# Two edits in a four-pass feed-forward kernel: the transposed loads of the next pass are issued after the gate stage, and the weight casts come in batches of 20 instead of 16

## The reference

```
x = layernorm(x + conv(x, filt))          # a 2048-tap filter along the sequence, D = 1024
g = silu((x @ w1.T) * s1) * ((x @ w2.T) * s2)      # 1024 -> 4096
u = gelu((g @ h1.T) * sh1)                         # 4096 -> 4096
v = gelu((u @ h2.T) * sh2)                         # 4096 -> 4096
out = layernorm(x + (v @ w3.T) * s3)               # 4096 -> 1024
```

## Time and profile before

| | us |
|---|---|
| time, median of 3 runs (lowest, highest) | 3886.93 (3883.72, 3892.93) |
| time of the profiled execution | 3908.22 |
| span of its slowest core, core 1 | 3906.7 |
| PE busy on core 1 | 2880.8 (74%) |
| ACT, DVE, POOL busy | 296.8, 722.2, 491.3 |

### The profile page before, as it was taken

How to read it: one execution, slowest core, us unless ns; L and a number is a source line. 1 busy time by engine, 2 the same in 40 slices (tenths; PEclk the granted TensorE clock), 3 DMA queues, 4 the chain that set the end, 5 groups by cost and what they waited for, 6 DMA issues and landing times.

```text
span 3906.7 us, 39367 instructions; the slowest of 8 cores (3860.7 to 3906.7 us)
## 1 busy us (share of the span) xinstructions
PE 2880.8 (74%) x13920; PEld 1382.7 (35%) x13920; DVE 722.2 (18%) x1397; ACT 296.8 (8%) x461; POOL 491.3 (13%) x890
## 2 busy tenths in 40 slices
PE   0534352443258555999699999969999978999995
PEld 0211121121023222444444444634444463444444
DVE  4333333333312221000320000041000022000003
ACT  0000000000011000000011000011000102110100
POOL 2233343333301222000000000000000000000000
PEclk9876676776679777999899999989999999999986
DMA  5787887887856998444453434434444453444432
GB/s 161 206 241 209 240 250 230 260 236 229 262 149 222 288 288 251 151 151 151 136 174 137 155 150 155 153 139 162 151 151 151 151 162 141 153 156 149 156 131 76
DMA packets 321267, 709.02 MB, mean 181 GB/s; under 512 B 72800, under 2 KB 236704, under 8 KB 294448
## 3 DMA queue, kind: packets, MB, share of 16 engines
q1 hardware_dynamic: 93440, 398.50, 29.3%
q0 software_dynamic: 80176, 207.28, 18.2%
q10 hardware_dynamic: 147456, 100.73, 8.5%
HBM read 588.91 MB, written 113.25 MB: 180 GB/s over the span
## 4 chain that ended last, share of the span: by engine, by line
PE 59%; DMA 22%; DVE 7%; issue 4%; POOL 3%; ACTq 2%; DVEq 2%; ACT 1%; SPq 0%; POOLq 0%
PE ps L166 56%; DMA wstgf<-h 9%; DMA h2s<-wstgb 6%; DMA wstgf<-w 4%; PE ps L164 3%; DMA w3s<-wstgb 2%; POOL x1bf L365 2%; ACTq L252 2%; DVEq L60 2%; DVE wstgb L238 2%; DMA xstg<-x 1%; DVE stats L292 1%; POOL wstgf L233 1%; DVE sqs L295 1%; DVE sqs L293 1%
## 5 line engine op out<-in xcount | busy, mean ns | idle before, releaser
L166 PE MATMUL ps<-gT,hsl 128*128 128x512 bf16 x3968 | 900.8, 386 | 149.2 <-ACT uT L471 144.7
L166 PE MATMUL ps<-uT,hsl 128*128 128x512 bf16 x3968 | 888.7, 383 | 4.3 <-ACT uT L471 4.3
L166 PE MATMUL ps<-xwh,Fh 128*128 128x512 bf16 x544 | 226.2, 416 | 610.5 <-DVE xwl L279 610.5
L166 PEld LDWEIGHTS ps<-gT,hsl 128*128 128x128 bf16 x3968 | 392.8, 99 | 638.7 <-issue 187.7
L166 PE MATMUL ps<-x1T,wsl 128*128 128x512 bf16 x1792 | 436.8, 384 | 217.5 <-DMA wsl<-w2s 118.7
L166 PEld LDWEIGHTS ps<-uT,hsl 128*128 128x128 bf16 x3968 | 390.6, 98 | 482.0 <-issue 43.2
L238 DVE CAST wstgb<-wstgf 128x512 bf16<-128x512 f32 x704 | 302.2, 429 | 734.5 <-DMA wstgf<-h 334.8
L529 DVE TENSOR_TENSOR y<-ps,s3bt 128x256 f32<-128x256 f32 x64 | 27.2, 425 | 1852.1 <-PE ps L164 1852.1
L233 POOL DMA_DIRECT2D wstgf<-h x512 | 288.2, 567 | 552.2 <-DVE wstgb L238 488.5
L166 PEld LDWEIGHTS ps<-x1T,wsl 128*128 128x128 bf16 x1792 | 176.9, 99 | 435.2 <-issue 229.9
L540 POOL DMA_DIRECT2D tmpf<-x1f x16 | 8.4, 528 | 2337.6 <-DVE y L545 1936.2
(11 more groups left out here) (52 smaller groups left out, 712.6 us busy)
## 6 DMA issues: line engine op xcount, KB each, us to landing
wstgf<-h POOLq DMA_DIRECT2D x512, 256.0 KB, 5.2
hsl<-h1s SPq DMA_DIRECT2D x64, 2048.0 KB, 9.4
hsl<-h2s SPq DMA_DIRECT2D x64, 2048.0 KB, 9.3
wstgf<-w POOLq DMA_DIRECT2D x192, 256.0 KB, 5.8
h2s<-wstgb ACTq DMA_DIRECT2D x512, 64.0 KB, 4.6
wsl<-w1s SPq DMA_DIRECT2D x32, 1024.0 KB, 6.3
wsl<-w2s SPq DMA_DIRECT2D x32, 1024.0 KB, 7.3
hsl<-w3s SPq DMA_DIRECT2D x16, 2048.0 KB, 9.5
```

The source lines that it names most:

```text
L166: sc.run("tensor", lambda t, a=lt, b=rh, o=out_ap, s=st: t.matmul(o, a, b, start=s, stop=False))
```

## The change

The eight transposes of L403 become a function, emit_x1T(q). It is called once ahead of the passes, and for pass q + 1 between the gate stage and the u stage of pass q. And the batch in the u stage of pass 0 is 20 jobs instead of 16: eight blocks get 20 jobs, the ninth gets 15, and the last seven get none.

```diff
     emit_casts_until("w2")
 
-    for q in range(NQ):
+    def emit_x1T(q):
         sc.waits("sync", x1T_slot.r)
         x1T_slot.r = []
         sc.wait("sync", (s_x1bst[0], s_x1bst[0].n))
         sc.wait("sync", (s_x1bst[1], s_x1bst[1].n))
         for ic in range(D // 128):
-            e = sc.run("sync", lambda s, ic=ic, q=q: s.dma_start(x1T[:, ic * TQ:(ic + 1) * TQ], x1bf[ic][q * TQ:(q + 1) * TQ, :], transpose=True), inc=s_tx1, k=16)
+            sc.run("sync", lambda s, ic=ic, q=q: s.dma_start(x1T[:, ic * TQ:(ic + 1) * TQ], x1bf[ic][q * TQ:(q + 1) * TQ, :], transpose=True), inc=s_tx1, k=16)
         x1T_slot.w = (s_tx1, s_tx1.n)
+
+    emit_x1T(0)
+    for q in range(NQ):
 
         for ob in range(HID // 512):
             sl = ob % 2
...
+        if q + 1 < NQ:
+            emit_x1T(q + 1)
+
         if q == 0:
             emit_casts_until("h1")
         uT_w_new = [None] * NOG
         for ob in range(HID // 256):
             sl = ob % 2
             if q == 0:
-                emit_casts(16)
+                emit_casts(20)
             sc.waits("sync", cast_grp_ev("h1", ob, 256))
             sc.waits("sync", hsl_slot[sl].r)
             hsl_slot[sl].r = []
```

## The result

The change makes the kernel slower: 1.0192 times the time of before, 95% interval 1.0166 to 1.0219. On the median of before that is +75 us, with an interval of 65 to 85; the forecast was +77. Leaving out the executions in which a die of the chip ran at a lower clock, which happened with either kernel and in the first profile of the changed one, its five other executions took 3954 to 3976 us; the forecast was 3964.

A forecast was written before the change was run, and what follows sets the result against it. PE was taken to set the end from 1550 us on, with casts pacing pass 0's u stage until then. 46.4 us for passes 1 and 2 plus 31 for pass 0 made 77, so 3887 became 3964, range 3930 to 3995.

The forecast's parts named there:

- Part 1: Pass boundaries: removing the hidden transposes and starting w1 and w2 loads sooner gives back 0; the 33 us stall stays.
- Part 2: Gate to u stage, passes 1 and 2: h1 loads wait behind the transposes on SP's queue; 23.2 us each, 46.4 together.
- the 22.4 us from transpose to matmul: Start of u stage, passes 1 and 2: first transpose to first matmul, taken about mid-range between 19.9 and 24.3 us.
- Part 3: Start of pass 0's u stage: PE's late start is covered by the first batch of 20 casts; 0, bound 10 us.
- Part 4: U stage of pass 0, batches of 20: cast phase ends 3 us later, two more blocks follow for 27.6; +31 us.
- The load's price, 6.6: Cast phase of pass 0: each 2 MB h1 load costs 6.6 us, from a fit of the gelu intervals.
- The sum: Whole kernel: 46.4 for passes 1 and 2 plus 31 for pass 0, 77 us slower, 3964 us, +2.0%.
- A: Pass boundaries: the stall is owed to late x1T and w1/w2 loads, the move gives back up to 99 us, 3865; 4%.
- B: U stage starts: the move is free as h1 loads get through in time, only part 4 is left, 3918; 4%.
- C: Pass 0: the larger batch costs nothing, the cast phase shrinks by as much as the tail grows, 3933; 11%.
- D: Pass 0: h1 load starved by casts, first batch doesn't cover it, transposes cost their full 12.6 us, 3981; 11%.
- E: Moved transposes: they run at the skill page's bandwidth, an estimated 4.0 us for eight, not the queue's pace, 3948; 3%.

The follow-up runs named there:

- after_c: The changed kernel, unedited, in a second profile on one chip beside a profile of the kernel before; u stage of pass 0 419.1 us against 390.8.
- move_after_two: Kernel after with batches of 16 and the transposes issued behind the u stage's first two h1 loads; ratio 1.0013 (0.9981 to 1.0045).
- move_only: Kernel after with the batch put back to 16, so only the transposes are moved; ratio 1.0154 (1.0062 to 1.0246).
- batch32_only: Kernel before with batches of 32 casts instead of 16, nothing moved; ratio 1.0044 (1.0011 to 1.0076).
- half_loads: Kernel before with the h1 loads of blocks 2 to 15 in pass 0 halved; u stage of pass 0 359.7 us against 390.8.
- the wait alone: Kernel before with SP waiting for the last gate matmul ahead of the h1 loads, transposes left at the pass head; ratio 1.0055 (1.0023 to 1.0088).
- before_c: The kernel before, unedited, profiled on one chip beside the changed kernel; u stage 390.8 us in pass 0, 222.3 in passes 1 to 3.
- the first four variants: Transposes moved only, batches of 20 only, transposes behind two h1 loads, SP's wait only; ratios 1.0154, 1.0012, 1.0013, 1.0055.

## Why the prediction was right, point by point

- **Part 1, nothing gained at the pass boundary:** right. The stall stayed at 32.7 to 33.1 us three times on every core of after_c, and so it did in the three variants of the move.
- **Part 2, the transposes stand ahead of the h1 loads on an in-order queue:** right in its mechanism, shown by move_after_two, where against move_only nothing but that order differs and the cost in passes 1 and 2 goes. The size was 12% too high: 20.6 and 20.8 us instead of 23.2. The term that was off is the 22.4 us from transpose to matmul, taken from the start of pass 0: in the rows of core 5 it was 10.2 us of issuing, not 11.6 to 12.6, and 9.6 for the load, together 19.8 (19.6 in the mean of the cores). Why the start of pass 0 is slower wasn't tried; that DMA there still carries other traffic is a guess. The slow restart was 2.1 us, forecast 1.8.
- **Part 3, the start of pass 0 covered by casts:** right, by 2 to 5 us. In the mean of the cores PE's two groups were done 45.1 us after the gate stage (forecast 38 to 48) and the first batch 48.5 us after it (forecast 52). PE's gap was 29.0 us, not 22.4, as an h1 load took 14.7 us from issue to the first matmul beside the casts and 9.1 in passes 1 and 2; only the allowance for contention, for which the prediction had no row, kept the forecast inside. With 16 jobs (move_only) the cover is gone by 2.8 us.
- **Part 4, the batch:** right. The cast phase was to end 3 us later; it ends 0.8 us later in the mean of the cores (319.2 and 318.4 us), which the spread of some 20 us between cores doesn't tell from 3 or from 0. The two more blocks behind it were to cost 27.6 us and cost 27.7. In all +28.3, forecast +31. By batch32_only's 5.8 us for each block moved out of the cast phase, an estimate gives the batch some 12 of the 28.3 and leaves 17 for the move (forecast 12 and 19); no run measured the two halves beside the kernel before on one chip. The load's price, 6.6, was a fit with two unknowns; half_loads puts it at 5.7. The 6 us for the transposes' traffic beside the casts is shown by no run by itself.
- **The sum:** 28.3 + 20.6 + 20.8 = 69.7 us of stage lengths, and +75 (65 to 85) by time, forecast 77. The 69.7 lies inside the interval, so there may be no rest to explain; the start of the second part differs by 10 to 20 us from core to core. The terms of all three passes erred to the same side, so the sum isn't right by cancelling.
- **The rivals:** A, B, C and D didn't come. E, eight transposes in 4 us, didn't either: they took 10 to 17 us on the queue, and with them ahead of the loads a pass lost 20.7 us against 11.4 for the wait alone.

## What to carry to other kernels

Before a DMA is issued earlier, look at what it waits for: on an in-order queue its wait is passed on to every load behind it. Here eight transposes that were hidden became 21 us a pass by standing ahead of two prefetches, and cost passes 1 and 2 nothing two places further down. And background work that paces a stage should be cut so thin that the foreground fits between, and be spread over the stages that have room: with casts in batches of 16, 20 or 32 PE idles and then has blocks left to do alone. Batches of 11 with all jobs still in the stage gain 39 us; with 5 to a block and the rest in the gate and v stages the casts are nearly hidden and the kernel is 4% faster than before. How much of the last step is thinness and how much the smaller share of jobs wasn't tried apart.

## What the runs showed of the hardware that wasn't expected

- A 2 MB load of h1 takes 13.2 us (median, before_c, core 1) from issue to landing among the casts, 9.6 over the whole kernel; it delays five-buffer casts by some 5.7 us, not by its own length.
- In the kernel before, most intervals of the cast phase alternated between 22 and 36 us although all had the same work; with half loads they lie between 22 and 31 on the slowest core, and with batches of 20 the full ones are 34 to 37. Which load falls in which interval would explain that, but it wasn't tried by itself.
- On the chip of the first four variants the first part took some 16 us longer than on the others, in all four kernels profiled there. A stage length is safely compared only with one from the same chip.
